# Cross-attention and a mixture of experts on one core: maxima moved behind the values in four steps of a batch, six steps of maxima ahead of the first exponent scores, x loaded batch by batch

## The chip, the core and the metric

The kernel runs on one core of a Trainium2 chip. The core has a matrix engine (PE, with its weight loads PEld), a vector engine (DVE), an activation engine (ACT), GpSimd (POOL) and SyncE (SP), which here only issues DMAs. They run side by side and wait for each other through semaphores. The metric is device time in microseconds (us) of one execution. Matmuls read from SBUF and write to PSUM; DVE and ACT read PSUM.

## What is computed

```python
x = x + xattn(layernorm(x), ctx, ctx)        # x: (8, 256, 512); ctx: (8, 256, 512)
x = x + ffn(layernorm(x))                    # router, 32 experts, the best 4 of a token

def xattn(q, k, v):                          # 32 query heads, 8 groups of keys, head size 16
    qh, kh, vh = q @ Wq.T, k @ Wk.T, v @ Wv.T
    attn = softmax(qh @ kh.T / 4)
    return (attn @ vh) @ Wfc.T + bfc
```

The change touches the attention alone, the first 37% of the time. The router and the experts follow it and are as they were.

## The kernel before

`attention` handles 8 batches (`NB`) of 256 tokens. A batch has 32 heads, taken in 16 steps `j` of two heads (`J`). x lies in SBUF as 16 tiles of 128 tokens (`NT`), two of them (`TT`) a batch.

Each head's scores are computed twice. `scores_for_max(b, j)` (L624) makes scores of a step's two heads with the queries on the partitions, into the two PSUM buffers `s1` (s in the trace); `row_max` (L470, DVE) reduces each to its row maxima `mx`. `scores(b, j)` (L638), "the exponent scores", makes them again, transposed and with the maximum already subtracted, into one of three buffers `stp`; `exponentials` (L348, ACT) writes their exponentials `pt`. `values(b, g)` (L654) multiplies two steps' exponentials with V into `ov`, and `ov_evac` (L332, ACT) empties `ov` after each second of them.

The maxima run ahead of the exponent scores: by 8 steps (`LEAD`). Four steps of maxima are one chunk (`CH`). `transpose_max` (L660, PE) turns a chunk, `split_max` (L478, L480, DVE) makes two bf16 halves `nm` and raises `mt_empty`, `stack_max` (L207, SP) copies them by four small DMAs into the rows of `qst` that `scores` reads. `scores` of the first step of a chunk waits for them.

Two waits tie PE to DVE: matmuls into an `s1` buffer wait until its last contents are reduced (`max_done`). Two tie it to ACT: `scores` waits for a free `stp` (`exp_done`), and `values` for its exponentials and, at every second one, for an emptied `ov` (`ov_empty`).

Nothing is scheduled automatically. Each engine's program is written out: PE does in step j `scores`, then `side_items` (projections, transposes and output of neighbouring batches), then the maxima of `maxima_of(b, j)`, then `late_items` (a transpose in steps 6, 10 and 14), then `values`, then `last_items`. `values` stands in every even step.

SP's queue at the start of a batch's loop holds, in this order, `stack_q(b + 1)` (six DMAs of q, L186), `stack_max` of the chunk that DVE splits in step 1, `stack_k(b + 1)` (six DMAs of k, L193), `stack_max` of step 5, and the next context. SP issues them one after the other and waits in front of the ones whose data aren't there.

x is loaded in four groups (`X_BEGINS`): batches 0, 1 and 2 by SP at the start, the other five in one DMA of 2560 KB from ACT's queue (L363), with Wfc and its bias behind it (L364, L365). DVE's `moments(b + 3)` (L410, L413), the layer norm's statistics for a later batch, stands in step 4 of batch b, between the reductions of steps 3 and 4. `add_bias` on POOL waits for Wfc and its bias.

Of the kernel before, what the change touches and what calls it, by code (L numbers as in the profile page):

```python
# [17 lines left out]
NB, S = 8, 256  # L18
TT = S // P
NT = NB * TT  # L20
# [3 lines left out]
DMA = 16  # L24
# [4 lines left out]
ROWS_QK = 6 * DH  # L29
ROWS_ST = ROWS_QK + 2  # L30
PLACES = 6
ROWS_OF_Q = ((0, 1, 2), (3, 4), (5,))
ROWS_OF_K = ((0, 3, 5), (1, 4), (2,))
X_BEGINS = (0, 2, 4, 6)
LEAD = 8
CH = 4
NC = J // CH
STP = 3
# [3 lines left out]
def attention(nc, x_in, ctx_in, wq, wk, wv, wfc, bfc, xs, st_new, ident):  # L42
# [3 lines left out]
    with ExitStack() as ctx:  # L46
# [6 lines left out]
        Bfc = sb("Bfc", [P, D], F32)  # L53
# [74 lines left out]

        def maxima_of(b, j):

            if b == 0 and j < LEAD - CH:
                return [(0, CH + 2 * j), (0, CH + 2 * j + 1)]
            at = b * J + j + LEAD
            return [(at // J, at % J)] if at < NB * J else []

# [9 lines left out]
        def _(sp):  # L145
# [42 lines left out]
            def stack_k(b, n):  # L188

                sp.wait_ge((k_hi, k_mid, k_lo)[n], b + 1)  # L190
                for at in ROWS_OF_K[n]:
                    dst = kst[b % 2][at:ROWS_QK:PLACES, :, :].rearrange("p g t -> p (g t)")
                    sp.dma_start(dst, k3[b % 2][:, n, :]).then_inc(k_stacked, DMA)  # L193
# [19 lines left out]
            for b in range(NB):  # L213
                for j in range(0, J, CH):
                    if j == 0 and 0 < b < NB - 1:
                        for n in range(3):
                            stack_q(b + 1, n)
                    if chunk_at(b, j) < NB * NC:
                        stack_max(chunk_at(b, j))
                    if j == 0 and b == 0:  # L220
                        for n in range(3):
                            stack_q(1, n)
                    if j == 0 and b < NB - 1:
                        for n in range(3):
                            stack_k(b + 1, n)
                    if j == CH:
                        next_ctx(b + 2)

# [54 lines left out]
        def _(act):  # L283
# [76 lines left out]
            k_first(1)  # L360
            x_evac(1, 0)
            x_evac(1, 1)
            act.dma_start(xs[:, X_BEGINS[3]:NT, :], xv[:, X_BEGINS[3]:NT, :]).then_inc(x_loaded[3], DMA)  # L363
            act.dma_start(Wfc[:, :, :], wfc).then_inc(w_loaded, DMA)  # L364
            act.dma_start(Bfc[:, :], bfc).then_inc(w_loaded, DMA)  # L365
            q_first(1, 0)
            deviations(2)

# [30 lines left out]
        def _(dve):  # L399
# [5 lines left out]
            def moments(b):  # L405

                if b * TT in X_BEGINS:
                    dve.wait_ge(x_loaded[X_BEGINS.index(b * TT)], DMA)
                for t in range(b * TT, b * TT + TT):
                    dve.bn_stats(st6[:, t, :], xs[:, t, :]).then_inc(stats, 1)  # L410
                for t in range(b * TT, b * TT + TT):
                    dve.wait_ge(stats, t + 1)
                    m = dve.bn_aggr(mv[:, t, :], st6[:, t, :])  # L413
                m.then_inc(var_ready, 1)
# [40 lines left out]
            def q_split(b, n):  # L455

                dve.wait_ge(q_hi, q_counts(b, n) + 1)
                if b == 1:
                    dve.wait_ge(q0_lo, 2 * n + 2)
                else:  # L460
                    dve.wait_ge(q_lo, q_counts(b, n) - 1)
                dve.tensor_tensor(qres[n][:, :], side[:, :], q_parts(b, n)[0], ALU.subtract).then_inc(qp_empty, 1)
                dve.wait_ge(qp_empty, q_counts(b, n) + 1)
                dve.tensor_copy(q_parts(b, n)[1], qres[n][:, :]).then_inc(q_mid, 1)  # L464
# [8 lines left out]
            def split_max(n):  # L473

                dve.wait_ge(mt_full, n + 1)
                if n >= 2:
                    dve.wait_ge(m_ready[n % 2], n // 2 * 4 * DMA)
                dve.tensor_scalar(nm[n % 2][:, 0, :], turn[0:4 * CH, 0:P], -1.0, None, ALU.mult).then_inc(mt_step, 1)  # L478
                dve.wait_ge(mt_step, n + 1)
                dve.scalar_tensor_tensor(nm[n % 2][:, 1, :], turn[0:4 * CH, 0:P], -1.0, nm[n % 2][:, 0, :],  # L480
                                         ALU.mult, ALU.subtract).then_inc(mt_empty, 1)
# [37 lines left out]
            row_max(0, 2)  # L519
            row_max(0, 3)  # L520
            split_max(0)
            moments(2)
            q_split(1, 0)
            refine(2)
            normalise(2, 0)
            normalise(2, 1)
# [39 lines left out]
        def _(pe):  # L566
# [272 lines left out]
            pe.wait_ge(xt_empty, 2 * TT)  # L839
            transpose_max(0)  # L840
            project_q(1, 0, range(C // 2, 2 * C))
            pe.wait_ge(kst_ready, 1)

            for b in range(NB):
                for j in range(J):
                    scores(b, j)
                    side_items(b, j)
                    for b1, j1 in maxima_of(b, j):
                        scores_for_max(b1, j1)
                    late_items(b, j)  # L850
                    if j == 0 and b:
                        values(b - 1, G - 1)
                    elif j and j % 2 == 0:
                        values(b, j // 2 - 1)
                    last_items(b, j)
            values(NB - 1, G - 1)
            pe.wait_ge(ovt_empty, NB * C - 1)
# [646 lines left out]
```

## Time and profile before

| | us |
|---|---|
| median of 3 runs | 1131.07 (1130.87 to 1133.53) |
| the profiled execution | 1135.69 |
| its span, first to last instruction | 1133.9 |
| attention (to the first instruction of the router) | about 427 |
| one batch of the attention, batches 1 to 5 | 47.2 to 47.4 |
| batch 0, with the entry | 96.2 |

All rows are of the profiled execution. A timeline row gives a start, a duration, the engine (SPq and ACTq are instructions that issue DMAs), the line, out<-in, shapes and a count, and in brackets how long the engine had been idle and what ended that. A row with a count of matmuls covers them from the first start to the last end. Batch b's first exponent scores start at 41.88 (b = 0), 96.21, then 143.3, 190.71, 238.08, 285.4, 332.83 and 373.27 us (b = 7).

### The profile page before, as it was taken

How to read it: one execution, taken by the hardware profiler on the slowest of the kernel's cores; microseconds unless marked ns; L12 is line 12 of the kernel's file. 1: busy time of each engine (PE TensorE's matmuls, PEld its weight loads, DVE VectorE, ACT ScalarE, POOL GpSimd, SP SyncE). 2: the span in 40 equal slices, each digit the busy share in tenths (PEclk: the TensorE clock that was granted, in tenths of full speed). 3: DMA queues.
4: the chain of work that ended last, by engine and by line, in shares of the span. 5: the costliest groups of instructions: out<-in, count | busy, mean ns of one | idle time of the engine just before them, and what ended most of it. 6: DMA issues, size and time to landing. Idle time of an engine off the chain costs nothing.

```text
span 1133.9 us, 19012 instructions
## 1 busy us (share of the span) xinstructions
PE 1032.1 (91%) x5518; PEld 664.7 (59%) x5520; DVE 418.6 (37%) x1039; ACT 349.3 (31%) x643; POOL 297.2 (26%) x387
## 2 busy tenths in 40 slices
PE   7689999999998979427999999999999999999995
PEld 6556666666665437215666666666665666666662
DVE  4476667766666524691111111111111111111110
ACT  2245454454545533141222222222222222222221
POOL 2101101011020000202344334334333344433432
PEclk9799999999999998757999999999999999999998
DMA  6433032130320003922765675675666667667443
GB/s 206 151 90 71 21 90 57 34 71 21 90 57 16 2 1 134 378 103 47 218 151 141 215 224 143 212 224 146 189 171 148 207 162 209 189 171 219 73 67 56
DMA packets 51449, 146.65 MB, mean 129 GB/s; under 512 B 9552, under 2 KB 18896, under 8 KB 47056
## 3 DMA queue, kind: packets, MB, share of 16 engines
q1 hardware_dynamic: 32192, 99.43, 26.3%
q0 software_dynamic: 17632, 42.74, 19.4%
q10 hardware_dynamic: 1584, 3.93, 1.0%
q8 instruction: 26, 0.43, 0.2%
q14 instruction: 15, 0.12, 0.0%
HBM read 100.73 MB, written 29.36 MB: 115 GB/s over the span
## 4 chain that ended last, share of the span: by engine, by line
PE 53%; issue 0%; DMA 0%; POOL 0%; ACT 0%; DVE 0%; POOLq 0%; ACTq 0%
PE y_ps L1420 18%; PE g_ps L1403 15%; PE u_ps L1403 15%; PE xt_ps L1396 3%; PE at_ps L1412 2%; DMA xg<-xd,gidx 0%; POOL out_x L1307 0%; ACT yb L1339 0%; ACT xT L1328 0%; DVE aT L1361 0%; ACT sg L1332 0%; DVE a L1374 0%; DVE a L1375 0%; POOL gidx L1290 0%; ACTq L1338 0%
## 5 line engine op out<-in xcount | busy, mean ns | idle before, releaser
L1420 PE MATMUL y_ps<-W,aT 128*128 x468 | 215.6, 597 | 1.1 <-DVE aT L1361 0.8
L1307 POOL DMA_INDIRECT out_x<-yb,yidx x78 | 125.3, 1606 | 297.2 <-DMA out_x<-yb,yidx 134.9
L348 ACT ACTIVATE pt<-stp 128x512 f32<-128x512 f32 x256 | 139.2, 597 | 169.4 <-PE stp L638 169.4
L470 DVE TENSOR_REDUCE mx<-s 128x2 f32<-128x512 f32 x256 | 163.0, 681 | 63.7 <-PE s L624 63.5
L1403 PE MATMUL g_ps<-W,xT 128*128 x624 | 183.3, 437 | 0.9 <-ACT xT L1328 0.9
L1403 PE MATMUL u_ps<-W,xT 128*128 x624 | 181.3, 434 | 0.0
L1403 PEld LDWEIGHTS u_ps<-W,xT 128*128 128x128 f32 x624 | 119.1, 191 | 49.9 <-issue 0.8
L1403 PEld LDWEIGHTS g_ps<-W,xT 128*128 128x128 f32 x624 | 113.5, 192 | 39.0 <-issue 2.4
L1374 DVE TENSOR_TENSOR a<-u_ps,sg 128x192 f32<-128x192 f32 x78 | 27.9, 358 | 291.5 <-ACT sg L1332 291.5
L1420 PEld LDWEIGHTS y_ps<-W,aT 128*128 128x128 f32 x468 | 83.5, 192 | 77.4 <-issue 77.3
L1332 ACT ACTIVATE sg<-g_ps 128x320 f32<-128x320 f32 x78 | 34.1, 437 | 306.2 <-PE u_ps L1403 306.2
L1361 DVE COPY aT<-at_ps 128x384 f32<-128x384 f32 x78 | 43.5, 558 | 183.3 <-PE at_ps L1412 183.3
L1339 ACT ACTIVATE yb<-y_ps,wt 128x512 f32<-128x512 f32 x78 | 53.7, 688 | 167.7 <-PE y_ps L1420 167.7
L624 PE MATMUL s<-kst,qst 96*128 96x256 bf16 x512 | 85.9, 277 | 20.4 <-DVE mx L470 19.6
L1293 POOL DMA_INDIRECT xg<-xd,gidx x80 | 80.9, 1011 | 69.8 <-POOL gidx L1290 65.8
L638 PE MATMUL stp<-qst,kst 98*128 98x256 bf16 x512 | 78.5, 276 | 8.5 <-DMA qst<-nm 8.2
L624 PEld LDWEIGHTS s<-kst,qst 96*128 96x128 bf16 x512 | 44.3, 98 | 61.8 <-DVE mx L470 41.2
L638 PEld LDWEIGHTS stp<-qst,kst 98*128 98x128 bf16 x512 | 45.2, 98 | 42.3 <-issue 33.6
L1290 POOL COPY gidx<-tok 128x1 uint32 (+1 forms) x80 | 58.4, 731 | 40.3 <-POOLq L895 29.6
L654 PE MATMUL ov<-pt,vx 128*32 128x256 f32 x1024 | 68.5, 385 | 0.0
L682 PE MATMUL side<-Wfc,oT 128*128 128x512 f32 x128 | 61.9, 599 | 1.5 <-ACT oT L338 1.5
L261 POOL TENSOR_TENSOR q<-qres,q 128x512 bf16<-128x512 f32 x14 | 16.2, 1158 | 161.7 <-DVE q L464 161.7
(172 smaller groups left out, 949.5 us busy)
## 6 DMA issues: line engine op xcount, KB each, us to landing
W<-in_wts SPq DMA_DIRECT2D x32, 2048.0 KB, 8.2
qst<-q SPq DMA_DIRECT2D x42, 256.0 KB, 4.9
ctxT<-in_ctx SPq DMA_DIRECT2D x8, 512.0 KB, 3.5
xd<-r_xn SPq DMA_DIRECT2D x16, 256.0 KB, 2.0
out_x<-xs SPq DMA_DIRECT2D x1, 4096.0 KB, 13.9
kst<-k SPq DMA_DIRECT2D x48, 64.0 KB, 2.1
xs<-in_x ACTq DMA_DIRECT2D x1, 2560.0 KB, 11.2
qst<-nm SPq DMA_DIRECT2D x128, 2.0 KB
```

What stands on the lines that cost most here:

```text
L348: act.activation(pt[g % 2][:, 2 * (j % 2) + r, :, :], stp[n % STP][:, :, :], ACT.Exp, scale=DH ** -0.5).then_inc(exp_done, 1)
L470: dve.tensor_reduce(mx[j // CH % 2][:, h:2 * G:G], s1[r][:, :, :], AX.X, ALU.max)\
L624: m = pe.matmul(s1[r][:, t, :], qst[b % 2][0:ROWS_QK, head(j, r), t * P:(t + 1) * P], kst[b % 2][0:ROWS_QK, head(j, r) // C, :], start=Tru ...
L638: m = pe.matmul(stp[n % STP][:, t, :], kst[b % 2][0:ROWS_ST, head(j, r) // C, t * P:(t + 1) * P], qst[b % 2][0:ROWS_ST, head(j, r), :], st ...
L654: m = pe.matmul(ov[c * VW:(c + 1) * VW, g % 2, :], vx[b % 2][:, t, g % 2 * C + c, :], pt[(b * G + g) % 2][:, c, t, :], start=(t == 0), sto ...
L682: m = pe.matmul(side[:, :], oT[t][:, c, :], Wfc[:, c, :], start=(c == 0), stop=(c == C - 1))
L1290: pool.tensor_copy(idx[p][:, :], tok[:, bass.ds(s, 1)]).then_inc(idx_ready, 1)
L1293: pool.indirect_dma_start(xg[p][:, :], None, xd[:, :], bass.IndirectOffsetOnAxis(idx[p][:, :], 0))\
L1307: pool.indirect_dma_start(out[:, :], bass.IndirectOffsetOnAxis(yidx[p][:, :], 0), yb[p][:, :], None, compute_op=ALU.add).then_inc(y_added, ...
L1339: act.activation(yb[p][:, :], y_ps[:, :], ACT.Copy, scale=wt[p][:, :]).then_inc(y_empty, 1)
L1403: m = pe.matmul(ps_[p][:, 0:IW], xT[p][:, c, :], W[:, bass.ds(buf, 1), (2 * c + g) * IW:(2 * c + g + 1) * IW] .rearrange("p a f -> p (a f) ...
L1420: m = pe.matmul(y_ps[:, :], aT[p][:, c, :], W[:, bass.ds(buf, 1), GW + c * D:GW + (c + 1) * D].rearrange("p a d -> p (a d)"), start=(c == ...
```

## The change

`VALUES_FIRST = (0, 6, 10, 14)`: in these steps PE does scores, side items, values, late items, and only then the maxima. In all other steps the order is as before.

Six steps of maxima instead of four (`ENTRY`) stand in front of the first exponent scores; steps 0 to 3 of batch 0 then hold one, two, two and one (`EARLY`) where they held two each. On DVE the two added reductions stand in front of `moments(2)`, behind `q_split(1, 0)`, which moves ahead.

x is loaded in eight groups of 512 KB. Those of batches 3 to 7 are issued by SP, each in batch b = 0 to 4 for batch b + 3, behind `stack_k(b + 1)`. Wfc and its bias are issued by SP in batch 0, behind x of batch 3. The three DMAs on ACT's queue are gone.

```diff
+VALUES_FIRST = (0, 6, 10, 14)
-X_BEGINS = (0, 2, 4, 6)
+X_BEGINS = tuple(range(0, NT, TT))
+ENTRY = 6
+EARLY = ((6,), (7, 8), (9, 10), (11,))
...
-            if b == 0 and j < LEAD - CH:
-                return [(0, CH + 2 * j), (0, CH + 2 * j + 1)]
+            if b == 0 and j < len(EARLY):
+                return [(0, m) for m in EARLY[j]]
...
+                    if j == 0 and b + 3 < NB:
+                        load_x(b + 3)
+                    if j == 0 and b == 0:
+                        sp.dma_start(Wfc[:, :, :], wfc).then_inc(w_loaded, DMA)
+                        sp.dma_start(Bfc[:, :], bfc).then_inc(w_loaded, DMA)
...
-            act.dma_start(xs[:, X_BEGINS[3]:NT, :], xv[:, X_BEGINS[3]:NT, :]).then_inc(x_loaded[3], DMA)
-            act.dma_start(Wfc[:, :, :], wfc).then_inc(w_loaded, DMA)
-            act.dma_start(Bfc[:, :], bfc).then_inc(w_loaded, DMA)
...
+            q_split(1, 0)
+            for j in range(CH, ENTRY):
+                row_max(0, j)
             moments(2)
-            q_split(1, 0)
...
+            for j in range(CH, ENTRY):
+                scores_for_max(0, j)
...
-                    for b1, j1 in maxima_of(b, j):
-                        scores_for_max(b1, j1)
-                    late_items(b, j)
+                    if j not in VALUES_FIRST:
+                        for b1, j1 in maxima_of(b, j):
+                            scores_for_max(b1, j1)
                     if j == 0 and b:
                         values(b - 1, G - 1)
                     elif j and j % 2 == 0:
                         values(b, j // 2 - 1)
+                    late_items(b, j)
+                    if j in VALUES_FIRST:
+                        for b1, j1 in maxima_of(b, j):
+                            scores_for_max(b1, j1)
                     last_items(b, j)
```

PE in steps 6 and 7 of batch 1; the names are s for the maxima's scores, stp for the exponent scores, ov for values, turn<-ident,o for the transpose of o. Before:

```order
L638 MATMUL stp<-qst,kst 128x256 x4
L624 MATMUL s<-kst,qst 128x256 x4
L673 MATMUL turn<-ident,o 128x128 x4
L654 MATMUL ov<-pt,vx 32x256 x8
L638 MATMUL stp<-qst,kst 128x256 x4
```

Changed:

```order
L645 MATMUL stp<-qst,kst 128x256 x4
L661 MATMUL ov<-pt,vx 32x256 x8
L680 MATMUL turn<-ident,o 128x128 x4
L631 MATMUL s<-kst,qst 128x256 x4
L645 MATMUL stp<-qst,kst 128x256 x4
```

Values and the transpose now stand between the exponent scores of step 6 and the maxima's scores; nothing stands between these and the exponent scores of step 7.

SP's queue in batch 1, from the q copies of the next batch to the next context. Before:

```order
L186 DMA qst<-q 16x8x1024 x6
L207 DMA qst<-nm 1x8x128 x4
L193 DMA kst<-k 16x8x256 x6
L207 DMA qst<-nm 1x8x128 x4
L152 DMA ctxT<-in_ctx 128x1024
```

Changed:

```order
L189 DMA qst<-q 16x8x1024 x6
L210 DMA qst<-nm 1x8x128 x4
L196 DMA kst<-k 16x8x256 x6
L152 DMA xs<-in_x 128x2x512
L210 DMA qst<-nm 1x8x128 x4
L155 DMA ctxT<-in_ctx 128x1024
```

The load of x stands behind six k copies, which stand behind the four copies of maxima that DVE's split in step 1 releases.

PE at the entry, from the projection for batch 1 into steps 0 and 1 of batch 0. Before:

```order
L593 MATMUL side<-xnT,Wq 128x256 x6
L638 MATMUL stp<-qst,kst 128x256 x4
L593 MATMUL side<-xnT,Wq 128x256 x8
L578 MATMUL turn<-ident,xn 128x128 x4
L624 MATMUL s<-kst,qst 128x256 x8
L638 MATMUL stp<-qst,kst 128x256 x4
```

Changed:

```order
L600 MATMUL side<-xnT,Wq 128x256 x6
L631 MATMUL s<-kst,qst 128x256 x8
L645 MATMUL stp<-qst,kst 128x256 x4
L600 MATMUL side<-xnT,Wq 128x256 x8
L585 MATMUL turn<-ident,xn 128x128 x4
L631 MATMUL s<-kst,qst 128x256 x4
L645 MATMUL stp<-qst,kst 128x256 x4
```

Eight matmuls for the maxima stand ahead of the first exponent scores, and four fewer behind them.

## Rows read from the trace of the kernel before

**Rows 1.** The page: busy time of each engine, and one DMA issue.

```profile
PE 1032.1 (91%) x5518; PEld 664.7 (59%) x5520; DVE 418.6 (37%) x1039; ACT 349.3 (31%) x643; POOL 297.2 (26%) x387
...
xs<-in_x ACTq DMA_DIRECT2D x1, 2560.0 KB, 11.2
```

**Rows 2.** Stretches: us, PE busy, PEld, DVE, ACT, POOL, granted clock, DMA share, GB/s.

```profile
27.70:31.10 3.40, 3.18 (x15) 2.49 (x16) 1.75 (x4) 0.82 (x2) 0.67 (x1) 0.51 0.33 80
...
44.70:51.50 6.80, 5.07 (x31) 3.76 (x31) 3.46 (x6) 2.16 (x4) 0.00 (x0) 1.00 0.00 0
51.50:58.40 6.90, 6.54 (x32) 5.09 (x31) 2.63 (x5) 1.67 (x3) 3.59 (x3) 0.51 0.00 0
...
190.70:238.08 47.38, 45.47 (x366) 30.27 (x365) 32.41 (x68) 23.47 (x46) 5.45 (x5) 1.00 0.23 54
```

**Rows 3.** Waits, 0 to 400 us: in total, times, longest.

```profile
PE s L624 <- DVE mx L470: 19.6, 63, 0.8
...
PE stp L638 <- DMA qst<-nm: 6.7, 2, 6.3
```

**Rows 4.** Timeline of batch 3, its steps 1 to 7.

```profile
195.64 2.77 SPq L207 DMA_DIRECT2D qst<-nm  x4
...
198.45 3.83 SPq L193 DMA_DIRECT2D kst<-k  x6
...
201.97 1.27 DVE L410 BATCH_NORM_STATS2 st<-xs 128x6 f32<-128x512 f32 x2
...
203.37 1.26 DVE L470 TENSOR_REDUCE mx<-s 128x2 f32<-128x512 f32 x2
...
205.79 0.27 PE L660 MATMUL turn<-ident,mx 128*128 128x128 f32 x1
...
206.34 0.60 PE L638 MATMUL stp<-qst,kst 98*128 98x256 bf16 x4
...
206.53 0.59 ACT L332 COPY xo<-ov 128x512 f32<-128x512 f32 x1
206.62 1.27 DVE L470 TENSOR_REDUCE mx<-s 128x2 f32<-128x512 f32 x2
...
207.35 0.39 PE L624 MATMUL s<-kst,qst 96*128 96x256 bf16 x2 [0.41 <-DVE mx L470]
...
207.94 0.39 PE L624 MATMUL s<-kst,qst 96*128 96x256 bf16 x2 [0.20 <-DVE mx L470]
...
208.18 0.60 PE L673 MATMUL turn<-ident,o 128*128 128x128 f32 x4
```

**Rows 5.** Timeline of SP alone, batch 1.

```profile
103.70 4.95 SPq L193 DMA_DIRECT2D kst<-k  x6
```

**Rows 6.** Timeline of the start; DMA issues in 209 to 216 us, size, us to landing.

```profile
0.81 0.45 SPq L149 DMA_DIRECT2D xs<-in_x  x1
...
4.19 1.29 DVE L410 BATCH_NORM_STATS2 st<-xs 128x6 f32<-128x512 f32 x2 [2.94 <-DMA xs<-in_x]
...
ctxT<-in_ctx SPq DMA_DIRECT2D x1, 512.0 KB, 3.5
```

**Rows 7.** Timeline of batch 3's step 10 and batch 4's step 0.

```profile
221.29 1.28 DVE L470 TENSOR_REDUCE mx<-s 128x2 f32<-128x512 f32 x2
...
239.41 0.11 PEld L624 LDWEIGHTS s<-kst,qst 96*128 96x128 bf16 x2 [0.35 <-DVE mx L470]
```

**Rows 8.** Timeline of batch 0.

```profile
41.88 1.01 PE L638 MATMUL stp<-qst,kst 98*128 98x256 bf16 x4 [6.28 <-DMA qst<-nm]
...
59.38 2.67 SPq L207 DMA_DIRECT2D qst<-nm  x4
...
66.21 4.76 SPq L193 DMA_DIRECT2D kst<-k  x6
...
70.80 0.60 PE L638 MATMUL stp<-qst,kst 98*128 98x256 bf16 x4
```

**Rows 9.** Timeline of ACT in batch 6, step 5.

```profile
346.09 0.59 ACT L332 COPY xo<-ov 128x512 f32<-128x512 f32 x1
```

## The prediction

> **What bounds the kernel now.** The page shows PE busy 91% of the span and no other engine over 37% [rows 1]. In a middle batch of the attention PE is busy 45.47 of 47.38 us [rows 2], so there only PE's waits and PE's clock are to be had. The list of waits names the waits: PE for DVE's reductions, 19.6 us over the attention in 63 pieces, and PE for the small DMAs of maxima, 6.7 us in two pieces [rows 3], nearly all of it at the entry [rows 8]. The third view is the granted clock by stretches: 0.51 (the level of 1.2 GHz) in stretches of 3.4 and 6.9 us early in batch 0, and 1.00 (2.4 GHz) in the middle batches [rows 2]. The experts' part is untouched; I carry it over.
>
> **The maxima behind the values.** In step 6 of batch 3 the exponent scores start at 206.34. A pair of matmuls takes 0.24 (207.94 to 208.18), so four take about 0.44 and the maxima's scores could start at 206.78 and end at 207.22. They start at 207.35, their second pair at 207.94, and the next work at 208.18: DVE only began the last two reductions at 206.62, 0.64 us each [rows 4]. Lost: 208.18 - 207.22 = 0.96 us. Between these maxima and those of step 5 PE has nothing but four matmuls; behind them stand values and a transpose. The change moves these forward, and 1.0 + 0.44 us of work covers the wait. Steps 10 and 14 have the same shape and the same 0.96. In step 0 the wait is smaller: 0.35 us in the weight loads [rows 7], of which I count 0.23.
>
> What takes the place of each wait:
> - Step 6: `values` needs `ov` emptied, and ACT does that from 206.53 to 207.12 [rows 4]. PE would reach the values at 206.78 and wait until about 207.24 (0.12 for the signal). Gain 0.96 - 0.4 = 0.55 us, unless PE comes late for another reason; then ACT is done, and it is 0.96.
> - Step 10: DVE puts two instructions for the output and two for the division ahead of the reductions, which start at 221.29 [rows 7] with or without the change. PE, 0.95 us earlier, meets them in step 11: the second reduction ends at 221.29 + 1.28 = 222.57, and the pair that needs it would have started at 222.28. Gain 0.54.
> - Step 14: ACT and DVE are done. Gain 0.96.
>
> Per batch 0.23 + 0.55 + 0.54 + 0.96 = 2.3 us, or 2.7 where step 6 counts in full. In batches 6 and 7 there are fewer side items; ACT empties `ov` until 346.09 + 0.59 = 346.68 in step 5 [rows 9], so steps 6 and 14 give 0.35 each, step 10 nothing, step 0 0.45: 1.15 and 0.8 us. These counts are bounded below by nothing (ACT holds every one of the values back) and above by 3 x 0.96 + 0.35 = 3.2 a batch; I take the walk through the steps.
>
> **The load of x.** This is the term that speaks against the change. Until now x of batches 3 to 7 came in one piece at 31 us, long before it was needed. Now DVE's `moments(b + 3)` in step 4 waits for a load that SP issues in step 2 to 3 of the same batch. In batch 3 SP issues the maxima's four copies from 195.64 and the six k copies from 198.45 to 202.28 [rows 4]; the load of x is behind them, at 202.3. A transfer of 512 KB takes 3.5 us to land when alone, and the very first x tiles, of this size too, are issued at 0.81 and let DVE start at 4.19, 3.4 later, with five more loads queued behind them [rows 6]. So x lands at 205.8, where DVE wants it at 201.97 [rows 4].
>
> The Trainium skill (DMA: Bandwidth & Descriptors, Anatomy of one DMA) fits a fixed 2.0 us plus bytes over 436 GB/s, an estimate of 3.2 us for this load, for DMAs issued by GpSimd. By it each stall would be 0.2 to 0.3 us shorter, 1 us in all; I stay with the rows.
>
> Behind the waiting DVE stand the reductions of step 4, and PE's maxima of step 5 wait for them. Moments take 203.37 - 201.97 = 1.40, a reduction 0.64, the signal 0.1: first pair at 205.8 + 2.15 = 207.95, second 0.65 later, and exponent scores of step 6 at 208.83, instead of 206.34: 2.5 us lost in batch 3, likewise in 4. In batch 1 the k copies are 4.95 us long [rows 5], 1.1 more than in batch 3, in batch 2 0.9 more: 3.65 and 3.4. Behind the stall step 6 counts its full 0.96 (ACT is done). Batches 1 to 4: stalls 3.65 + 3.4 + 2.5 + 2.5 = 12.05, gains 4 x 2.69 = 10.8; sum +1.3 us.
>
> **Entry and batch 0.** The exponent scores of step 0 start at 41.88 after a wait for the maxima's copies [rows 8], which share the engines with 2560 KB of x [rows 1] and Wfc. Without this load the copies land about 4 to 5 us after the split, at 38 to 39 us. The two added steps of maxima take the time until then, held by DVE: I get 39.1 for the first scores, 2.8 earlier. Two steps of maxima fewer in steps 0 and 3, with their waits, give some 3 more. So the copies of 59.38 [rows 8] are issued at about 53.5. From there, though, the old queue counts: four copies, six q, six k copies up to 66.21 + 4.76 = 70.97 [rows 8], 11.6 us after 59.38, then x, 3.4, then moments, reductions and matmuls, 3.0. The scores of step 6 would start 18.1 us after the copies, at 71.6, where they start at 70.80 now [rows 8]. All the gain of the entry is given back to this one wait, of some 9 us on DVE and 7 to 8 on PE: +0.8 us. Step 10 gives 0.3, step 14 is taken up by the copies ahead of batch 1: -0.3.
>
> Wfc and its bias cost nothing: they land by about 72, and POOL's `add_bias` delays only `q_third` by a few us, whose result is stacked a batch later. Three fewer DMAs on ACT's queue save nothing, ACT waits there.
>
> **The clock.** A stall of 7 us in batch 0 and four of 2 to 3 us are of the kind that lowers PE's clock: it fell for 51.5 to 58.4 after a stretch in which PE was busy 5.07 of 6.80 us [rows 2]. At the lower level four matmuls take 1.01 us [rows 8] instead of 0.60 [rows 4]. Low stretches are 3.4 to 6.9 us long [rows 2]; half the speed for 3.4 costs 1.7. Batch 0: +1.6, since PE works through the rest of a low stretch. Batches 1 and 2 fall nearly surely, 3 and 4 about every other time: 2.8 x 1.7 = +4.8, between 0 and 10.
>
> **Sum** on the span of the profiled execution, which ran 4.6 us over the median with its launch; I apply the difference to the median: batch 0 +0.8 - 0.3 + 1.6, batches 1 to 4 +1.3, clock +4.8, batches 5 to 7 -(2.3 + 1.15 + 0.8) = -4.25. Total +3.95: **1135.0 us**. 0.3%, about what a measurement can tell from no change, is 3.4 us.
>
> **Rivals.**
> - **The clock holds in batches 1 to 4.** Then +3.95 - 4.8 = -0.85: 1130.2. For it: each stall leaves PE idle only from 206.06 to 207.95. Against: the fall at 51.5 needed no longer wait. The Trainium skill (TensorE: Matmul & The Clock Gate, What's actually happening) has the clock fall after an idle stretch; by that rule PE, never idle for long there, would keep 2.4 GHz, and this rival would hold. The row at 51.5 does not bear the rule out as it stands.
> - **x is there in time** (the other side, faster). If SP came to the load 3.8 us earlier than I read, DVE would not stall. It decides where x lands before 201.97, that is issued by 198.5, just where the k copies begin [rows 4]. Then the entry keeps 5.8 + 0.3, each of batches 1 to 5 has 2.3, 6 and 7 1.95: -19.6, 1111.5. Against: the order of SP's queue is fixed, and its first wait is for a split by DVE. Half of it (shorter stalls, clock held) would be 1120 to 1127.
> - **ACT becomes the bound of the values.** All moved `values` wait for ACT as in step 6. The gains of batches 1 to 4 shrink from 2.69 to 1.0 each: +6.8, 1142. For it: ACT ends late in steps 6 of batches 0, 3, 6. Against: after the stall ACT has time.
> - **The entry does not do what it says**: if the maxima's copies at 33.7 are slow for another reason than x, the first scores stay at 41.9, and batch 0 ends 2.8 later: 1137.8, within the forecast.
>
> **How the numbers follow.** Forecast (stalls, and low clock after most of them) 0.55, with 1132.5 to 1139 its own range; clock holds 0.26; x in time or nearly so 0.09; ACT bound 0.10. The range 1129 to 1140.5 leaves out x in time, most of ACT bound and little else. Faster by over 0.3% (below 1127.7): 0.09, and 0.01 of the others, 0.10. Slower (above 1134.5): 0.36 of the forecast's 0.55, 0.10 of ACT bound, 0.46. Within: 0.44. Slower is only just the likelier.
>
> **What would show it.** In the changed trace: DVE waiting for xs about 4 us ahead of L415 in batches 1 to 4 and about 9 in batch 0; the first exponent scores near 39; no wait of PE for a reduction in steps 6, 10 and 14 of batches 1 to 5; batch 5 at 45.1 us instead of 47.4, batches 1 to 4 at 47 to 50; low clock in stretches behind each stall. A batch 3 under 46 us would refute the stall; clock 1.00 from 80 us on makes it the first rival; first scores at 41.9 the last.

## The result and the profile after

The changed kernel takes **1139.68 us** (median of 6 runs, 1138.20 to 1142.57) against 1130.95 (1130.36 to 1133.53) of the kernel before on the same chip. The ratio is 1.0077, with a 95% interval of 1.0062 to 1.0092: slower, by 8.7 us. That lies inside the predicted range of 1129.0 to 1140.5 and on the side that was held the likelier, but the predicted loss was 3.95 us, less than half.

The profiled execution of the changed kernel ran 1138.22 us (span 1136.5, granted clock 0.953; before 1135.69, 1133.9 and 0.961). The page has nearly the same busy times as [rows 1]:

```profile
PE 1030.8 (91%) x5519; PEld 668.4 (59%) x5520; DVE 418.5 (37%) x1039; ACT 349.8 (31%) x643; POOL 297.2 (26%) x387
```

The work has not grown, so the difference lies in waits and clock. The list of waits from 0 to 400 us (total, times, longest) now has DVE waiting for x, which it did before only at the start, and PE's own wait for the reductions, 19.6 us in 63 pieces of 0.8 at most [rows 3], has turned into a few long ones:

```profile
DVE st L415 <- DMA xs<-in_x: 30.9, 6, 9.3
...
PE s L631 <- DVE mx L475: 29.0, 30, 7.4
```

30.9 us of DVE's waiting for x are the five stalls that the prediction counted on (9.26, 4.84, 4.57, 4.50, 4.86 in batches 0 to 4) and the 2.9 us at the start that were there before [rows 6]. The timeline of batch 3 shows one of them from end to end; its columns are start, duration, engine, line, operation, and in brackets the idle time ahead and what ended it:

```profile
199.27 3.81 SPq L196 DMA_DIRECT2D kst<-k  x6
...
203.13 0.59 SPq L152 DMA_DIRECT2D xs<-in_x  x1
...
206.61 0.27 PE L667 MATMUL turn<-ident,mx 128*128 128x128 f32 x1
...
207.37 1.29 DVE L415 BATCH_NORM_STATS2 st<-xs 128x6 f32<-128x512 f32 x2 [4.50 <-DMA xs<-in_x]
...
208.78 1.26 DVE L475 TENSOR_REDUCE mx<-s 128x2 f32<-128x512 f32 x2
...
209.50 0.39 PE L631 MATMUL s<-kst,qst 96*128 96x256 bf16 x2 [2.62 <-DVE mx L475]
...
210.10 0.39 PE L631 MATMUL s<-kst,qst 96*128 96x256 bf16 x2 [0.21 <-DVE mx L475]
...
210.33 0.60 PE L645 MATMUL stp<-qst,kst 98*128 98x256 bf16 x4
```

Read down: SP is through with the k copies at 203.1 and only then issues x; x lets DVE start at 207.37, 4.2 us later; moments, aggregate and one reduction later PE gets its first pair of matmuls, after 2.62 us without work. Before, DVE never waited there [rows 4].

A batch is measured from its first exponent scores to those of the next, and step 5 and step 6 in the same way. In us, from the two profiled executions (up to batch 6, the changed kernel's clock is low ahead of its first scores and in batches 0, 3 and 4):

| | start to b1 | b1 | b2 | b3 | b4 | b5 | b6 | b7 to end |
|---|---|---|---|---|---|---|---|---|
| before | 96.21 | 47.14 | 47.37 | 47.37 | 47.38 | 47.37 | 40.44 | 760.65 |
| after | 95.74 | 48.16 | 47.88 | 49.59 | 51.02 | 44.94 | 39.05 | 760.08 |
| difference | -0.47 | +1.02 | +0.51 | +2.22 | +3.64 | -2.43 | -1.39 | -0.57 |
| predicted, without the clock of b1 to b4 | +2.1 | +0.96 | +0.71 | -0.19 | -0.19 | -2.3 | -1.15 | -0.8 |
| step 5, before and after | | 2.29, 5.81 | 2.29, 5.53 | 2.29, 5.46 | 2.29, 6.00 | 2.29, 2.29 | | |
| step 6, before and after | | 3.37, 2.46 | 3.37, 2.47 | 3.37, 3.53 | 3.37, 4.62 | 3.37, 2.76 | | |

(Step 6 of batch 0, whose step 5 lasts 10.39 us, took 2.93 before and 3.69 after; the table's columns start with batch 1.)

The granted clock in the same stretches (columns as in [rows 2]): batches 3, 4 and 5, then the low stretches inside batches 3 and 4.

```profile
191.78:241.37 49.59, 46.59 (x367) 31.41 (x364) 32.49 (x68) 23.57 (x46) 5.44 (x5) 0.97 0.25 62
241.37:292.39 51.02, 47.88 (x366) 31.91 (x364) 32.50 (x68) 23.57 (x46) 5.45 (x5) 0.93 0.23 59
292.39:337.34 44.95, 44.56 (x367) 30.61 (x365) 29.85 (x59) 23.09 (x44) 5.93 (x6) 1.00 0.24 60
211.60:215.00 3.40, 3.40 (x22) 2.41 (x15) 2.45 (x5) 1.36 (x3) 1.16 (x1) 0.50 0.19 33
259.40:266.20 6.80, 6.74 (x38) 3.86 (x39) 4.58 (x10) 2.12 (x4) 1.16 (x1) 0.50 0.24 78
```

Batch 5, which has the moved maxima and no stall, is 2.4 us shorter than before and PE is busy 44.56 of 44.95 us in it (45.47 of 47.38 in [rows 2]). Batches 1 to 4 are longer than before although they save the same waits: in the changed trace PE waits for no reduction in steps 6, 10 and 14 of batches 1 to 5.

The profiled executions differ by 2.5 us and the medians by 8.7. The profiled one of before was 4.7 us above its median, that of after is one of its two fastest. Part of this scatter has nothing to do with the change: from the start of batch 7 to the end, seven kernels of this study run the same program, and their traces need between 756.5 and 763.1 us there. The first 70 us scatter too. The kernel with the values alone (below) has the same program as before up to step 6 of batch 0, but its trace reaches that step at 66.60 us, where before's reached it at 70.80 [rows 8]: 2.5 us are gained ahead of the first scores, at 39.39 for 41.88, and most of the rest in step 2, which takes 5.57 us for 6.84. Before's own trace had the clock at 0.51 there [rows 2]; no other trace of the study has it low between 52 and 58 us. Timeline of the values alone, then its step 2 by windows:

```profile
66.60 0.60 PE L639 MATMUL stp<-qst,kst 98*128 98x256 bf16 x4
```

```profile
52.15:57.72 5.57, 4.41 (x43) 2.80 (x40) 3.86 (x8) 1.92 (x4) 1.10 (x1) 1.00 0.00 1
```

So medians are used for the size of a thing, and traces for its place.

### The profile page after: what moved, and what is told of

Read it like the earlier page. It is cut to its first block, busy times and chain, and to the rows that moved or that the text cites. A ratio compares the mean times of both kernels' runs of the same rounds, so it can differ in the third digit from the quotient of the medians.

```text
span 1136.5 us, 19017 instructions
## 1 busy us (share of the span) xinstructions
PE 1030.8 (91%) x5519; PEld 668.4 (59%) x5520; DVE 418.5 (37%) x1039; ACT 349.8 (31%) x643; POOL 297.2 (26%) x387
## 4 chain that ended last, share of the span: by engine, by line
PE 53%; DMA 1%; issue 0%; ACT 0%; POOL 0%; DVE 0%; POOLq 0%; ACTq 0%
PE y_ps L1433 17%; PE g_ps L1416 15%; PE u_ps L1416 15%; PE xt_ps L1409 3%; PE at_ps L1425 2%; DMA out_x<-yb,yidx 0%; DMA xg<-xd,gidx 0%; POOL out_x L1320 0%; ACT yb L1352 0%; ACT xT L1341 0%; ACT sg L1345 0%; DVE a L1387 0%; DVE a L1388 0%; POOL gidx L1303 0%; POOLq L1327 0%
## 5 line engine op out<-in xcount | busy, mean ns | idle before, releaser
L631 PEld LDWEIGHTS s<-kst,qst 96*128 96x128 bf16 x512 | 47.0, 99 | 65.1 <-DVE mx L475 42.2
L645 PE MATMUL stp<-qst,kst 98*128 98x256 bf16 x512 | 80.8, 282 | 2.0 <-DMA qst<-nm 1.9
L661 PE MATMUL ov<-pt,vx 128*32 128x256 f32 x1024 | 72.6, 403 | 2.4 <-ACT xo L340 2.4
L645 PEld LDWEIGHTS stp<-qst,kst 98*128 98x128 bf16 x512 | 48.4, 100 | 28.0 <-issue 17.7
L1425 PEld LDWEIGHTS at_ps<-ident,a 128*128 128x128 f32 x234 | 30.4, 141 | 43.8 <-issue 42.9
```

Of the source, the lines that this page charges most:

```text
L631: m = pe.matmul(s1[r][:, t, :], qst[b % 2][0:ROWS_QK, head(j, r), t * P:(t + 1) * P], kst[b % 2][0:ROWS_QK, head(j, r) // C, :], start=Tru ...
L645: m = pe.matmul(stp[n % STP][:, t, :], kst[b % 2][0:ROWS_ST, head(j, r) // C, t * P:(t + 1) * P], qst[b % 2][0:ROWS_ST, head(j, r), :], st ...
L661: m = pe.matmul(ov[c * VW:(c + 1) * VW, g % 2, :], vx[b % 2][:, t, g % 2 * C + c, :], pt[(b * G + g) % 2][:, c, t, :], start=(t == 0), sto ...
```

## Experiments

Ratios are to the kernel before on the same chip, with 95% intervals. In the names of the theories, "stall" is the one of the prediction: x lands late because its load stands behind the k copies, DVE waits, PE waits for DVE, and PE's clock falls behind it.

### The parts, alone and left out

**The loads alone** (before, with only the load of x and Wfc changed):

```diff
-X_BEGINS = (0, 2, 4, 6)
+X_BEGINS = tuple(range(0, NT, TT))
...
+                    if j == 0 and b + 3 < NB:
+                        load_x(b + 3)
+                    if j == 0 and b == 0:
+                        sp.dma_start(Wfc[:, :, :], wfc).then_inc(w_loaded, DMA)
...
-            act.dma_start(xs[:, X_BEGINS[3]:NT, :], xv[:, X_BEGINS[3]:NT, :]).then_inc(x_loaded[3], DMA)
...
```

> The kernel before with the change of the loads alone: x in groups of 512 KB on SP, Wfc late, nothing on ACT's queue. My theory: first exponent scores near 38 us instead of 41.9, scores of step 6 of batch 0 at 73 us (18.1 us after the maxima's copies of chunk 1) instead of 70.8; stalls of 3.7, 3.4, 2.5 and 2.5 us in step 5 of batches 1 to 4, and 0 to 6 us for lowered clock; 1145 to 1151 us, the slowest of the four. The rival (loads are harmless, the order costs): within 3 us of before.

Measured: 1151.42 us, ratio 1.0183 (1.0151 to 1.0215), +18.7 us after the 1132.70 of this chip. The batches 1 to 4 are 51.16, 53.23, 51.50 and 52.05 us, together 18.7 longer than before, and 5 and 6 are unchanged at 47.37 and 40.44. Step 5 grows by 3.16, 3.92, 2.71 and 3.58 (the stall), step 6 by another 0.86, 1.20, 0.97 and 1.10, and step 7 by 0.74 and 0.45 in batches 2 and 3 (the lower clock): 13.4 us of stall and 5.3 behind it. Each of the four batches has a low stretch; the one of batch 2:

```profile
166.20:173.00 6.80, 6.59 (x39) 4.00 (x39) 4.07 (x9) 2.62 (x5) 1.16 (x1) 0.50 0.22 78
```

At the entry, in the timeline of this kernel, the first exponent scores start 6.5 us sooner than in [rows 8], and the wait for x takes it all back: batch 1 begins at 96.14 here and at 96.21 before, in a trace of before that was itself late.

```profile
35.42 0.60 PE L640 MATMUL stp<-qst,kst 98*128 98x256 bf16 x4 [2.14 <-DMA qst<-nm]
...
66.60 1.29 DVE L412 BATCH_NORM_STATS2 st<-xs 128x6 f32<-128x512 f32 x2 [8.82 <-DMA xs<-in_x]
```

**The values alone** (before, with `VALUES_FIRST` and its order in the loop of steps, nothing else):

```diff
+VALUES_FIRST = (0, 6, 10, 14)
...
-                    for b1, j1 in maxima_of(b, j):
-                        scores_for_max(b1, j1)
-                    late_items(b, j)
+                    if j not in VALUES_FIRST:
+                        for b1, j1 in maxima_of(b, j):
+                            scores_for_max(b1, j1)
...
```

> The kernel before with the values ahead of the maxima in steps 0, 6, 10, 14 alone. My theory: batches 1 to 5 lose 2.3 to 2.4 us each, batch 6 1.3, batch 7 0.8, batch 0 0.3 to 1: about 14 us under before, 1117 us, clock column as before. The rival (values held by ACT in all these steps, or DVE as the next bound): less than 1 us a batch, 1125 us or more.

Measured: 1118.65 us, 0.9890 (0.9862 to 0.9918), -14.1 us. Batches 1 to 6 are short: 44.94, 44.95, 45.34, 44.95, 44.95 and 39.04.

**The entry alone** (before, with `ENTRY`, `EARLY` and DVE's new order):

```diff
+ENTRY = 6
+EARLY = ((6,), (7, 8), (9, 10), (11,))
...
+            q_split(1, 0)
+            for j in range(CH, ENTRY):
+                row_max(0, j)
             moments(2)
-            q_split(1, 0)
...
```

> The kernel before with the entry alone: six steps of maxima ahead of the first exponent scores, the loads in one piece from ACT's queue as before. My theory: the maxima stand in the wait for the copies at no cost and are missing in steps 0 and 3, but batch 0's step 8 is held by the copies of the maxima again: 1 to 3 us under before, batches 1 to 7 unchanged. The rival (it costs, since DVE's moments and PE's first scores come later): at or over before.

Measured: 1128.41 us, 0.9986 (0.9966 to 1.0007), from 10 runs. The point estimate is -1.8 us, which is not told apart from nothing.

**All but the loads** (the changed kernel with x in one piece at the entry, as before):

```diff
-X_BEGINS = tuple(range(0, NT, TT))
+X_BEGINS = (0, 2, 4, 6)
...
-                    if j == 0 and b + 3 < NB:
-                        load_x(b + 3)
...
+            act.dma_start(xs[:, X_BEGINS[3]:NT, :], xv[:, X_BEGINS[3]:NT, :]).then_inc(x_loaded[3], DMA)
...
```

> The changed kernel with x of batches 3 to 7, Wfc and its bias loaded as before, in one piece from ACT's queue at the entry; the orders of PE and DVE stay changed. My theory (the load of x behind the k copies makes DVE and PE stall, and lowered clock follows): no stall in step 5, batches 1 to 5 at 45.0 us instead of 48.2 to 51.0 (1 to 4) and 45.0 (5); batch 0 waits for the maxima's copies again, first scores near 41.9, but has two steps of maxima fewer behind them, some 3 us less; in all about 17 us under before: 1114 us. The rival (the new order on PE costs time, for instance by waits for ACT or by more clock falls, whatever the loads): batches 1 to 4 stay over 47 us and the time over 1131 us.

Measured: 1117.43 us, 0.9873 (0.9846 to 0.9900). Batches 1 to 5 take 44.94 or 44.95 us each. Against the changed kernel's 1.0077 that is 2.0%, some 23 us: the loads cost as much with the moved values as without them, or a little more.

**All but the values** (the changed kernel with the old order in PE's loop):

```diff
-                    if j not in VALUES_FIRST:
-                        for b1, j1 in maxima_of(b, j):
-                            scores_for_max(b1, j1)
+                    for b1, j1 in maxima_of(b, j):
+                        scores_for_max(b1, j1)
+                    late_items(b, j)
...
```

> The changed kernel with PE's order inside a step as before (maxima, late items, values in every step): loads and entry changed, values not. It completes the set: values alone gave -14 us, loads alone +19 to +21, both with the entry +8.7. If the parts only add, this is 14 to 15 us over the changed kernel, 1153 to 1155, that is 2 % over before, and steps 6 behind a stall are 3.4 us long (0.96 more than the 2.46 of the changed kernel) where the clock holds. If the order of the values costs anything in a stalled batch, the difference is smaller than 10.

Measured: 1156.54 us (1148.27 to 1159.29), 1.0199 (1.0161 to 1.0237). So the values are worth 1.0199 - 1.0077 = 1.2%, 14 us, in the changed kernel, the same 14 as alone. So the parts nearly add: the values -14 with or without the loads, the loads +19 alone and +23 beside the rest. The entry adds nothing beside the loads (1.0199 here, 1.0183 for the loads alone). -14 and +19 make +5 where +8.7 was measured, and each of the two is uncertain by 3 to 4 us; that the parts do more than add is neither shown nor excluded.

### The place in SP's queue

If the stall comes from the place of the load behind six k copies, one place earlier must remove it; the prediction put the point of decision at an issue by 198.5, just where the k copies begin. Wfc and its bias, which stand behind x in batch 0, move with it.

```diff
-                    if j == 0 and b < NB - 1:
-                        for n in range(3):
-                            stack_k(b + 1, n)
                     if j == 0 and b + 3 < NB:
                         load_x(b + 3)
...
+                    if j == 0 and b < NB - 1:
+                        for n in range(3):
+                            stack_k(b + 1, n)
```

> The changed kernel with the load of x (and in batch 0 Wfc and its bias) one place earlier in SP's queue, ahead of the six k copies instead of behind them. By my reading the load is then issued at 198.5 in the frame of batch 3 and lands at 202.0, where DVE wants it at 201.97: no stall in batches 1 to 4, all at 45.0 us; in batch 0 the load is issued at about 59.6 and lands at 63.1, DVE wants it at 57.9: a wait of 5 us instead of 9.3. About 1116 to 1118 us. If the place in the queue is not what counts, batches 1 to 4 stay over 47 us.

Measured: 1118.14 us, 0.9900 (0.9856 to 0.9943): 1.8%, 20 us under the changed kernel by swapping two neighbours in one queue. Timeline of its batch 3:

```profile
191.00 0.44 SPq L152 DMA_DIRECT2D xs<-in_x  x1
...
191.48 3.82 SPq L196 DMA_DIRECT2D kst<-k  x6
...
194.64 1.29 DVE L415 BATCH_NORM_STATS2 st<-xs 128x6 f32<-128x512 f32 x2
```

There are no brackets behind DVE's statistics: x landed just as DVE came to it. It was no more than just in time: in batches 1, 2 and 4 DVE waited 0.29, 0.26 and 0.58 us for it, which cost PE nothing. Batch 4 in the same timeline:

```profile
240.12 1.29 DVE L415 BATCH_NORM_STATS2 st<-xs 128x6 f32<-128x512 f32 x2 [0.58 <-DMA xs<-in_x]
```

Batches 1 to 5 are 44.94 to 44.95 us each; batch 3 by windows:

```profile
183.50:228.45 44.95, 44.55 (x367) 30.61 (x365) 32.58 (x68) 23.46 (x46) 5.43 (x5) 1.00 0.27 69
```

One long wait is left, in batch 0, where the copies of q stand ahead of the load as well; 5 us were expected of it and it was 7.64. The load was issued at 59.38, as expected, but took 5.8 us to land, not 3.5:

```profile
65.25 1.29 DVE L415 BATCH_NORM_STATS2 st<-xs 128x6 f32<-128x512 f32 x2 [7.64 <-DMA xs<-in_x]
```

### The clock behind the stall

The rival "the clock holds" and the forecast differ in 4.8 us. To take the clock away and leave the stall, PE was given extra exponent-score matmuls in step 5 of batches 1 to 4, ahead of the maxima for which it waits (their result is overwritten; they are work added, nothing is left out). First 14 of them:

```diff
+            def keep_busy(b):
+                n = b * H + 4 * (CH - 1)
+                pe.wait_ge(exp_done, n + 1 - STP)
+                for _ in range(14):
+                    pe.matmul(stp[n % STP][:, 0, :], kst[b % 2][0:ROWS_ST, head(CH + 1, 0) // C, 0:P],
+                              qst[b % 2][0:ROWS_ST, head(CH + 1, 0), :], start=True, stop=True)
...
+                    if j == CH + 1 and 1 <= b <= NB - 4:
+                        keep_busy(b)
```

> The changed kernel with 14 extra bf16 matmuls of 256 columns on PE (about 1.5 us, results overwritten by the exponent scores that follow) in step 5 of batches 1 to 4, ahead of the maxima that wait for DVE; the stall of DVE is as before. My theory of the clock term: the lowered clock behind the stalls of these batches costs 5 to 6 us of the changed kernel's time, and extra work that fills the stall takes it away: batches 1 to 4 at 47.2 to 48.3 us each, clock 1.00 from 75 us to the end of batch 5, 1134 us (5 to 6 under the changed kernel's 1139.7). The rival (the matmul stretches are long for another reason, or the stall alone makes the loss): 1139 to 1141 us, no faster than the changed kernel.

Measured: 1137.16 us (1134.08 to 1144.82), 1.0068 (1.0031 to 1.0105). The interval holds both the changed kernel's 1.0077 and the 1134 expected: inconclusive. Its trace says why. In batch 3 the 14 take 1.70 us and leave PE 1.60 us idle, and the clock still fell (low from 211.1 to 214.5); in batch 4 it held behind 1.91 us of idle time:

```profile
205.88 1.70 PE L654 MATMUL stp<-qst,kst 98*128 98x256 bf16 x14
209.18 0.39 PE L631 MATMUL s<-kst,qst 96*128 96x256 bf16 x2 [1.60 <-DVE mx L475]
```

So again with 24, which fill the stall. The edit is the same as above but for the number:

```diff
...
+                for _ in range(24):
...
```

> As e5 with 24 instead of 14 extra matmuls in step 5 of batches 1 to 4, 2.6 us of work, so that only about 1 us of each stall is idle on PE. e5 took the fall in batch 4 away but not in batch 3, and its time could not be told from the changed kernel's. If idle PE in the stall is what lowers the clock, no stretch of 0.5 stands between 75 us and the end of batch 5, batches 1 to 4 are 47.8 to 48.5 us each, and the time is 3 to 5 us under the changed kernel's 1139.7: 1135 to 1137. If it comes out at 1139 or more, the clock term of my sum was too large by itself.

Measured: 1134.28 us (1130.29 to 1138.43, 12 runs), 1.0027 (1.0011 to 1.0044). No interval touches the other: 1.0077 - 1.0027 = 0.5%, **5.6 us faster with 96 useless matmuls**. The trace still has the stall, with PE at work in it (idle for 0.35 us at most), step 6 at 2.46 or 2.47 in all four, and the clock at 1.00 from 76.7 to 377 us. Not all of the gain can be put down to the clock. Batches 1 to 4 are 5.95 us shorter than in the changed kernel's trace: 4.3 of this lie in steps 6 and 7, where the clock held, but 1.9 in step 5 (5.22, 5.61, 5.05 and 4.97 us for 5.81, 5.53, 5.46 and 6.00), since DVE waited 17.4 us for x in these batches and not 18.8. Nothing ties that to the extra matmuls. Timeline of batch 3, then three windows that roughly cover batches 2, 3 and 4:

```profile
207.56 2.78 PE L654 MATMUL stp<-qst,kst 98*128 98x256 bf16 x24
210.18 0.73 PE L631 MATMUL s<-kst,qst 96*128 96x256 bf16 x4
```

```profile
143.30:191.00 47.70, 47.19 (x389) 32.74 (x388) 32.48 (x67) 23.56 (x46) 5.18 (x6) 1.00 0.25 64
191.00:239.00 48.00, 47.56 (x390) 32.86 (x389) 32.48 (x67) 23.57 (x46) 5.59 (x6) 1.00 0.26 65
239.00:287.00 48.00, 47.84 (x391) 33.07 (x390) 32.47 (x67) 23.56 (x46) 5.98 (x6) 1.00 0.27 68
```

### A version without the stall

The room that the loads leave can be had by loading earlier: x of batch 3 behind the first copies of maxima, x of batch b + 4 in batch b behind the context.

```diff
+            load_x(3)
...
-                    if j == 0 and b + 3 < NB:
-                        load_x(b + 3)
...
                     if j == CH:
                         next_ctx(b + 2)
+                        if b == 0:
+                            sp.dma_start(Wfc[:, :, :], wfc).then_inc(w_loaded, DMA)
+                            sp.dma_start(Bfc[:, :], bfc).then_inc(w_loaded, DMA)
+                        if b + 4 < NB:
+                            load_x(b + 4)
```

> The changed kernel, but each group of x issued by SP where it has nothing else to do and long before its use: batch 3's right behind the first maxima's copies at the entry, batch b + 4's behind the context in batch b, Wfc and its bias behind the context in batch 0. My theory: no wait of DVE for x; first scores at 38.9, scores of step 6 of batch 0 about 6 us earlier than in the changed kernel, batches 1 to 5 at 45.0; 19 to 20 us under before, 1111 to 1112 us. If the loads still delay the small copies of maxima, batch 0 or the start of batches shows waits of PE for them, and the time is 1113 or more.

Measured: 1114.84 us (1111.22 to 1119.51), 0.9841 (0.9810 to 0.9873). Every batch from 1 to 5 takes 44.94 to 45.59. In batch 0 one wait of PE for the copies of maxima remains, 0.96 us in front of step 8, the scores of which then ran at the low clock; this is the sign that the expectation named for 1113 us or more:

```profile
67.13 1.03 PE L646 MATMUL stp<-qst,kst 98*128 98x256 bf16 x4 [0.96 <-DMA qst<-nm]
```

Then with Wfc and its bias behind x(3) at the entry as well, and in batch 7 the values ahead only in steps 0 and 6 (the edit against the changed kernel):

```diff
+            load_x(3)
+            sp.dma_start(Wfc[:, :, :], wfc).then_inc(w_loaded, DMA)
+            sp.dma_start(Bfc[:, :], bfc).then_inc(w_loaded, DMA)
...
-                    if j not in VALUES_FIRST:
+                    first = j in VALUES_FIRST and (b < NB - 1 or j < LEAD)
...
```

> The kernel of e4 with Wfc and its bias issued at the entry right behind x of batch 3 too (SP and the DMA engines are idle there until 52 us), and in batch 7 the values ahead of the maxima in steps 0 and 6 alone, since steps 10 and 14 of batch 7 have no maxima and the later transposes cost 0.6 us there. Theory: 0.5 to 2 us under e4, 1113 to 1114 us; the copies of maxima for step 8 of batch 0 land 0.3 us sooner.

Measured: **1112.10 us** (1110.10 to 1115.34), 0.9837 (0.9792 to 0.9882): the best of this study, 18 us under the kernel before and 2.4% under the changed one. It is not told apart from the version above it, and the copies for step 8 of batch 0 were not sooner: PE waits 1.29 us for them. Both versions have one thing worse than the changed kernel in their traces, batch 6 at 40.37 and 40.14 instead of 39.05, with a stretch of low clock. Six extra matmuls, of the kind of `keep_busy`, ahead of the maxima in steps 11, 12 and 13 of batch 6 were to hold the clock:

```diff
+                    if b == NB - 2 and j in (11, 12, 13):
+                        keep_busy(b, j, 6)
...
```

> The kernel of e8 with six extra matmuls ahead of the maxima of steps 11, 12 and 13 of batch 6, where PE waits for DVE and e8's trace shows the clock at 0.5 for 3.4 us (343 to 346). If the extra work fills the waits and the clock holds there, batch 6 is 39.0 us instead of 40.1 and the time 1 us under e8; if DVE's waits leave less room than 0.65 us a step, it is 1 us over.

Measured: 1114.14 us, 0.9854 (0.9821 to 0.9886). Batch 6 came down to 39.52, the clock fell in batch 7 instead, at 382.5, and the whole was not faster: the 1 us that was expected is missing, and the two versions are not told apart.

## Why the prediction was right or wrong

**The bound and the waits that the maxima leave.** Right. The values alone give 14.1 us; the walk through the steps had 5 x 2.3 + 1.15 + 0.8 = 13.45. The agreement is closer than it should be, since the 13.45 hold nothing for batch 0, where steps 6 to 15 were 1.0 us shorter in that trace; batches 1 to 6 gave 12.9 there for 12.65. In the changed kernel, batch 5 gains 2.43 where 2.3 was said, batch 6 1.39 for 1.15. By steps: step 6 goes from 3.37 to 2.76 without a stall (0.61 for the 0.55 that leaves ACT its time) and to 2.46 behind one (0.91 for 0.96); step 14 from 4.33 to 3.32 (1.0 for 0.96); steps 10 and 11 together gain 0.58 for 0.54; step 0 0.24 for 0.23. The rival in which ACT becomes the bound of the values is refuted by the same numbers: in batch 5's step 6 PE waits for it, but only 0.23 us, in the timeline of the changed kernel:

```profile
308.61 1.07 PE L661 MATMUL ov<-pt,vx 128*32 128x256 f32 x16 [0.23 <-ACT xo L340]
```

**The stall.** Right in place and cause: neither DVE nor the clock but one place in SP's queue decides, as the swap shows, and the rival "x is there in time" was priced rightly at 1111.5: the two versions that also spare batch 0 its wait measured 1112.1 and 1114.8, the swap, which keeps that wait, 1118.1. The size was right in batches 1 and 2 (3.52 and 3.24 for 3.65 and 3.4) and too small in 3 and 4 (3.17 and 3.71 for 2.5 each). The term that was too small there is the landing, for which the prediction took the row of a transfer that "takes 3.5 us to land when alone". The issues of the changed kernel at 202 to 208 us and at 252 to 259 us, with size and time to landing:

```profile
xs<-in_x SPq DMA_DIRECT2D x1, 512.0 KB, 4.2
```

```profile
xs<-in_x SPq DMA_DIRECT2D x1, 512.0 KB, 4.6
```

In batches 1 and 2 it was 3.6 and 3.8, in batch 0 4.0. What lengthens a landing is open. The place behind the k copies does not explain it by itself: in the 20 loads of batches 1 to 4 of the five kernels that have x there it was 3.4 to 4.6 us, and 3.4 to 3.7 in the one with 24 extra matmuls; ahead of the k copies it was 3.6 to 4.2. Issues of the kernel with 24 extra matmuls at 156 to 160 us and of the one with x ahead of k at 235 to 241 us:

```profile
xs<-in_x SPq DMA_DIRECT2D x1, 512.0 KB, 3.4
```

```profile
xs<-in_x SPq DMA_DIRECT2D x1, 512.0 KB, 4.2
```

The Trainium skill (DMA: Bandwidth & Descriptors, Anatomy of one DMA) gives, by its fit for DMAs issued by GpSimd, an estimate of 3.2 us for this size. All landings here, issued by SP, were longer, and the prediction's 3.5 was nearer to them. Two stalls of 0.67 and 1.21 us more make 1.9 us of the 4.7 that were missing in the medians. What the swap also shows is that the place decided and not the landing: with 3.6 to 4.2 us, x issued ahead of the 3.8 us of k copies came in time for PE, though with nothing to spare for DVE.

**Batch 0.** Over-charged by 2.6 us. The first scores came where they were said to (38.92 for 39.1), the wait for x was the 9 us that were said (9.26), PE's 7.38, and the scores of step 6 started at 70.25 where 71.6 was said:

```profile
69.26 1.20 PE L631 MATMUL s<-kst,qst 96*128 96x256 bf16 x4 [7.38 <-DVE mx L475]
...
70.25 1.06 PE L645 MATMUL stp<-qst,kst 98*128 98x256 bf16 x4
```

The working has the copies of maxima issued at 53.5; they were issued at 52.3. These 1.2 us are a low stretch that it carried over from before's trace: step 2 takes 6.84 us there and 5.57 or 5.58 in every other trace of the study. The other 1.2 lie behind step 6: step 14 and 15 together gained 0.6 where nothing was given them, steps 6 to 8 with the low clock cost 1.1 net for the 1.6 that were charged, and step 10 gained 0.4 for 0.3.

That the whole gain of the entry is given back to this wait was right: with the loads alone the first scores are 6.5 us earlier and batch 1 is 0.07 earlier. Since before's trace reached step 6 some 4 us late, the wait may well cost more than the entry gains. The 3.0 us by which the first scores start earlier are no sure gain of the change: the same entry begins them at 42.80 in the kernel without the values' order, and the old entry at 39.39 in that of the values alone.

**The clock.** Right in kind, near in size, wrong in where. 4.8 us (0 to 10) had been set for it in batches 1 to 4. With the 24 extra matmuls the ratio falls by 5.6 us, but the traces put only 4.3 us to the clock, 1.07 + 0.54 = 1.6 in batch 3 (step 6 at 3.53 for 2.46, step 7 at 2.73 for 2.19) and 2.16 + 0.52 = 2.7 in batch 4. "Batches 1 and 2 fall nearly surely, 3 and 4 about every other time" was the wrong way round in the profiled execution: 1 and 2 kept 2.4 GHz, 3 and 4 fell, for 3.4 and 6.8 us. Without the moved values the same stalls lowered it in all four batches, in both traces (the loads alone, and all but the values). Whether the moved values help the clock or it is a matter of the single execution isn't shown, with one trace of the changed kernel; its six executions do differ, with a mean granted clock of 0.946 to 0.956, 0.953 in the profiled one. The first rival, that the clock holds (1130.2), falls: it fell twice in that trace, and the median is 9.5 us above the rival's time.

The Trainium skill (TensorE: Matmul & The Clock Gate, What's actually happening) has the clock fall after an idle stretch, and the prediction read from it that PE, never idle for long in these stalls, would keep 2.4 GHz. The trace does not agree with that reading: PE was idle for 2.62 and 2.98 us ahead of the falls in batches 3 and 4, and for 2.96 and 2.69 in batches 1 and 2, where the clock held.

**The sum.** In the profiled executions the change costs 2.5 us, and the terms as measured make it: 95.74 - 96.21 = -0.47, then +1.02 + 0.51 + 2.22 + 3.64 - 2.43 - 1.39 - 0.57. Against the predicted 3.95, the landings of batches 3 and 4 put in 1.9, batch 0 took off 2.6, the clock of batches 1 to 4 (1.6 + 2.7 for 4.8) 0.5 and small terms 0.25: 2.5.

So the sum of the two traces came out near the forecast in part by luck: terms of 1.9 and 2.6 us were off in opposite directions. The medians are another 6.2 apart: the profiled execution of before was 4.7 over its median of 1130.95, that of after 1.5 under its own. The weakest step is therefore "I apply the difference to the median": it took one execution for the others. The larger part has a place: up to step 6 of batch 0, before's trace is 4.2 us behind another trace of the same program (70.80 and 66.60), about as much as it is over its median, though the medians' own executions have no trace to compare with. The clock can carry a part of the 1.5, since the profiled execution of the changed kernel had falls in two batches of four only, at about 2 us each, but no trace of a slower execution of it was taken. How the rest is shared between the clock in batches 1 and 2, the entry and the experts' part stays open. Two signs that had been named were slightly missed as well: batch 4 took 51.02 us where 47 to 50 was said for batches 1 to 4, and the clock was to be low behind each stall.

## What to carry to other kernels

- A transfer's time to be there is the time at which its queue comes to it plus its landing, and the first can decide: here six small copies ahead of one load, 3.8 us of issuing in batch 3, were the difference between a gain of 1.0% and a loss of 0.8%. Where a load is moved, write down the queue around its new place and when the queue's last wait before it is released; then swap it with its neighbour before anything else is tried.
- In an engine that works in strict order a wait that is put in is paid by what is queued behind it: not the moments of x, needed by nobody soon, but the reductions behind them stopped PE.
- One profiled execution is not the median. Before a difference of traces is applied to medians, compare the traces of two kernels over a stretch where their programs are the same: here 4.2 us lay in the first 70.
- A stall of the bound engine is paid twice where its clock falls afterwards; if the stall cannot go, work that fills it can be worth more than it costs.
- Between two dependent items the time of the work that stands there is what counts: the longest other work belongs into the shortest such gap.

## What the runs showed of the hardware beyond what was expected

- A load of 512 KB on SP's queue took 3.4 to 4.6 us to land right behind six copies of 64 KB (20 loads in five kernels), and 3.6 to 4.2 ahead of them (4 loads). Issued right behind Wfc and its bias it took 7.5 us once, in batch 0 of the first version without the stall.
- Idle times of PE of about 3 us, of one kind and in one trace, were followed by the lower clock in two cases and not in two others. With the 14 extra matmuls it fell once after 1.60 us of idle time and not after 1.91 in the next batch, and with the 24, which left 0.35 us idle at most, not once from 76.7 to 377 us. What sets the difference is open.
- With 96 matmuls whose results nobody reads the kernel was 0.5% faster; in its trace the clock accounts for 4.3 us of it.
- A program's first 40 us are not the same in each execution: the first exponent scores began at 39.39 and 41.88 us in two kernels with the same program up to there, and between 37.64 and 42.80 in five others with the same program.
